# A selective scan between two routed layers: DMA transposes for the normalised rows, and one product in sixteen moved to VectorE

## The chip, the cores and the metric

One core of a Trainium2 chip runs the whole program. The metric is the device time in microseconds; lower is better. Engines are named as in the profile: PE (TensorE matmul), PEld (its weight loads), DVE (VectorE), ACT (ScalarE), POOL (GpSimd), SP (SyncE, which here only issues DMAs).

## The reference

The input x is 2 x 2048 tokens of 1024 channels. Three residual layers follow each other, each on a layer-normalised input:

```python
x = x + 0.5 * ffn(layernorm(x))
x = x + scan(layernorm(x))
x = x + 0.5 * ffn(layernorm(x))

def ffn(x):      # A 64 x 16 x 1024, B 64 x 1024 x 16, W 1024 x 1024
    vecs = einsum('arh,bsh->bsar', A, x)
    _, idx = top_k(norm(vecs, axis=-1), 4)
    routes = one_hot(idx, 64).sum(-2) / 4
    v = einsum('bsa,bsar->bsr', routes, vecs)
    return x @ W.T + bias + einsum('bsa,ajr,bsr->bsj', routes, B, v)

def scan(x):     # 16 states a channel
    delta_r, B_mat, C_mat = split(x @ W_xproj.T)             # 128, 16, 16
    delta = softplus(delta_r @ W_dt.T + b_dt)
    h[t] = exp(delta[t] * A) * h[t-1] + delta[t] * B_mat[t] * x[t]
    return sum over states (h * C_mat) + x * D_param
```

## The kernel before, in words

A unit is one of the two ffn layers on 128 tokens: 32 units of kind 1 (first ffn) and 32 of kind 2 (second), 64 in a row, numbered from 0. A planner (`plan`) sets their order once: kind 1 first, then a mix, as the scan's results come. The scan runs underneath, in units 3 to 59: its work is 1024 blocks, and `block_at` deals them out over twentieths of a unit, so each engine's `unit` function is a fixed list in which `scans(lo, hi)`, `decays(lo, hi)`, `loads(a, lo, hi)` and `states(a, third)` are set between the steps of the ffn. No engine reorders anything; each waits on semaphores in its list's order.

The ffn on PE. The rows are split into a high and a low f16 part (`xT[:, 0]`, `xT[:, 1]`), and so are the weights. Each of the three products (`experts` into pv, `base` and `routed` into po) is 2 halves of the columns x 24 matmuls of 128x512: the first two "thirds" are high rows by both weight parts, the last third is low rows by the high weights. In unit a, PE does base(a), routed(a), then experts(b) of the next unit b = a.after. ACT squares the experts' result, DVE sums, takes the top four and makes the routed rows (`gather`), SP turns them by a DMA transpose into uT (`turn`, L409).

The normalised rows of b before the change. DVE takes statistics (`unit_stats`), ACT finishes them (`prepare`) and writes xn in f32 (`normed`, L842). PE transposes xn in eight blocks into PSUM (`norm_blocks`, L552) after the second third of routed(a, 1). ACT copies each half of the result to f16 (`high`, L847), DVE subtracts it from the f32 one for the low part (`low_part`, L1094). The experts of b wait for both (L625, L626). The same transposes also serve the scan's input (`scan_blocks`) and, in kind 2, the scan's output (`y_blocks`).

The scan. A tile is 512 token-channel columns; a chunk is 2 or 4 token blocks (`SIZES`), with two or one part a tile. A block i is one of a tile's 16 states; a group G is four blocks, g = G % 4. For each block ACT computes exp(delta * A) into pA in PSUM, two buffers (`decay`, L942); for each group POOL multiplies delta*x by B into Hr (`times_b`, L512 and L518). DVE runs the scan in place (L1157), ACT keeps the last column (`keep_last`, L928), POOL multiplies the group's 2048 columns by C in place (`times_c`, L528), PE sums over states (`sum_states`, L727). Four Hr buffers go round. Delta and delta*x of the next tiles come over HBM by SP's spreads (L354, L361), which wait until decays or `times_b` have freed their buffers.

Of the kernel before, what the change touches and what calls it, by code (L numbers as in the profile page):

```python
# [12 lines left out]
AHEAD = 10  # L13
LEAD = 14
# [105 lines left out]
def build(nc, x, AT, BT, WT, bias, WxT, WdtT, b_dt, A_log, D_par, out):  # L120
# [41 lines left out]
    with ctx:  # L162
# [43 lines left out]
        pjs = xn[:, 0:NX]  # L206
        drs = auxs[:, 0:P]
# [55 lines left out]
        s_xT = sem("s_xT"); s_xhi = sem("s_xhi"); s_xlo = sem("s_xlo")  # L263
        s_vec = sem("s_vec"); s_sq = sem("s_sq"); s_n2 = sem("s_n2"); s_mk = sem("s_mk"); s_gm = sem("s_gm")
# [38 lines left out]
        def _(sp):  # L303
# [106 lines left out]

            def loads(a, lo, hi):
# [28 lines left out]
            def unit(l, a, b):  # L440
# [22 lines left out]
                loads(a, 9, 18)  # L463
# [20 lines left out]
        def _(pool):  # L484
# [36 lines left out]
            def times_c(G):  # L521
                g = G % 4
                c = chunk_of_tile[G // 4]
                pool.wait_ge(s_sv, G + 1)
                pool.wait_ge(s_ldc[g], 16 * (c.q + 1))
                h = split(Hr[:, G % NH, :, :].rearrange("p s t -> p (s t)"), c)
                by_c = Cr[:, g, 0:c.width].unsqueeze(1).broadcast_to([P, 4 * c.parts, c.width])
                pool.tensor_tensor(h, h, by_c, ALU.mult).then_inc(s_cm, 1)  # L528
# [18 lines left out]
        def _(pe):  # L547
# [20 lines left out]
            def norm_blocks(b, half):  # L568
                if half == 0:
                    pe.wait_ge(s_xn, b.u + 1)  # L570
                if half == 0:
                    pe.wait_ge(s_u, b.u * 2)
# [33 lines left out]
            def first_base(a):  # L606
# [10 lines left out]
                for k in range(KD):  # L617
                    pe.wait_ge(s_loW, k + 1)
                    for nb in range(2):
                        nc.tensor.matmul(po[:, nb, :], xT[:, 0, k, :], wW[:, 1, k, nb * HF:(nb + 1) * HF],  # L620
                                         start=False, stop=False)
# [9 lines left out]
            def base(a, nb, third):  # L631
# [7 lines left out]
                product(po[:, nb, :], xT, wW, nb, third, False, False)  # L639
# [92 lines left out]
            def unit(l, a, b):  # L732
# [61 lines left out]
            norm_blocks(US[0], 0)  # L794
            norm_blocks(US[0], 1)
# [5 lines left out]
        def _(act):  # L801
# [37 lines left out]
            def normed(b, nT):  # L839
                act.wait_ge(s_nT, nT)  # L840
                act.wait_ge(s_pq, nT // 2)
                nc.scalar.activation(xn[:, :], xin[:, b.p, :], ACT.Identity, scale=lnb["ln1"]["r"][:, :],  # L842
                                     bias=lnb["ln1"]["nm"][:, :]).then_inc(s_xn, 1)

            def high(b, half):
                act.wait_ge(s_xT, b.u * 2 + 1 + half)
                nc.scalar.activation(xT[:, 0, half * KB:(half + 1) * KB, :].rearrange("p k t -> p (k t)"), ptn[half],  # L847
                                     ACT.Copy).then_inc(s_xhi, 1)
# [16 lines left out]
            def normed2(a, xT_done):  # L865
                act.wait_ge(s_xT, xT_done)
# [55 lines left out]
            def keep_last(G):  # L922
# [3 lines left out]
                src = split(Hr[:, G % NH, :, :].rearrange("p s t -> p (s t)"), c)[:, :, c.width - 1]  # L926
                dst = hst[:, 16 * k:16 * (k + c.parts)].rearrange("p (k c) -> p k c", c=16)[:, :, 4 * g:4 * g + 4]
                nc.scalar.activation(dst, src.rearrange("p (s k) -> p k s", s=4), ACT.Copy).then_inc(s_sv, 1)  # L928
# [16 lines left out]
            def unit(l, a, b):  # L945
# [25 lines left out]
                decays(4, 7)  # L971
# [3 lines left out]
                delta_copy(a, 0)  # L975
                if late:
                    projection_copies(late)
                decays(8, 9)
                delta_out(a, 0)
                if b:  # L980
                    prepare(b)
                decays(9, 10)
                if b:
                    normed(b, 2 * (a.f1s - (a.kind == 1)))
                decays(10, 12)
                if b:
                    high(b, 0)
                if b:
# [321 lines left out]
```

## Time and profile before

| | |
|---|---|
| median of 3 runs | 2722.13 us (2721.1 to 2724.64) |
| the profiled execution, its own time | 2721.68 us |
| its span | 2719.8 us, granted clock 0.987 |
| DMA moved | 390.29 MB |

The page shows busy time, share of the span and instruction count of each engine; a group row shows the line, engine and tiles, the count, the busy time in all and the mean of one in ns, and then the idle time just before them and what ended it. A timeline row begins with start and length in us. Matmuls overlap: their length is longer than the distance at which they follow each other, so cost on PE is read from start to start. L numbers are lines of the kernel before.

### The profile page before, as it was taken

Reading aid. Unit: us, or ns where it says so; the run is one execution under the profiler, and the core shown is the slowest. Engines: PE = TensorE matmul, PEld = TensorE weight load, DVE = VectorE, ACT = ScalarE, POOL = GpSimd, SP = SyncE. Lnnn points to the kernel's source line nnn. Section 1 sums busy time; section 2 is a strip of 40 time slices with the busy share of each in tenths; the row PEclk is TensorE's granted clock in tenths of the full one; section 3 lists DMA queues with packets and bytes.
Section 4 is the critical chain, followed back from the end, with each engine's and each line's share of the span. In section 5 each row is a group of like instructions: output and inputs, shape, how many; then the busy total and the mean of one; then the engine's idle time right before and its main releaser. Section 6 shows DMA issues by size and latency. Waiting matters only on the chain.

```text
span 2719.8 us, 39965 instructions
## 1 busy us (share of the span) xinstructions
PE 2593.5 (95%) x13664; PEld 1178.2 (43%) x13664; DVE 2227.7 (82%) x2933; ACT 1505.0 (55%) x3363; POOL 2350.0 (86%) x703
## 2 busy tenths in 40 slices
PE   4989999999989999999999999999999999999999
PEld 1444444444434444444444444444444444444444
DVE  8448888888878898888888988888888889989943
ACT  5347666665545555555556555555555555656521
POOL 2138998899999999999998999999999999999910
PEclk8989999999999999999999999999999999999999
DMA  5145444644464454645454455544555455554321
GB/s 223 52 117 154 144 148 135 172 141 144 131 183 150 136 156 130 190 141 147 139 177 139 147 153 156 157 130 147 156 172 149 134 156 161 159 144 150 103 63 54
DMA packets 333217, 390.29 MB, mean 143 GB/s; under 512 B 149459, under 2 KB 249939, under 8 KB 333014
## 3 DMA queue, kind: packets, MB, share of 16 engines
q1 hardware_dynamic: 316118, 354.18, 43.8%
q10 hardware_dynamic: 16896, 33.56, 4.0%
q8 instruction: 108, 1.77, 0.3%
q14 instruction: 95, 0.78, 0.1%
HBM read 250.82 MB, written 103.29 MB: 130 GB/s over the span
## 4 chain that ended last, share of the span: by engine, by line
PE 57%; DVE 16%; POOL 6%; DMA 6%; issue 5%; ACT 4%; DVEq 4%; ACTq 1%; SPq 0%; POOLq 0%
PE po L560 20%; PE pv L560 9%; PE po L564 9%; DVE mreg L1157 7%; PE py L727 6%; PE pv L564 4%; POOL mreg L518 3%; PE pv L689 2%; POOL mreg L528 2%; DMA delta_scratch<-mreg 2%; DVE sel L1114 2%; PE pv L708 1%; PE pv L552 1%; DVEq L1116 1%; DMA uT<-sel 1%
## 5 line engine op out<-in xcount | busy, mean ns | idle before, releaser
L528 POOL TENSOR_TENSOR mreg<-mreg 128x2048 f32<-128x2048 f32 x256 | 1163.0, 4543 | 70.7 <-ACT hst L928 70.0
L1157 DVE TENSOR_TENSOR_SCAN mreg<-pA,hst,mreg 128x512 f32<-128x512 f32 (+1 forms) x1024 | 1048.9, 1065 | 50.2 <-ACT pA L942 43.8
L942 ACT ACTIVATE pA<-mreg,nA 128x512 f32<-128x512 f32 (+1 forms) x1280 | 744.4, 598 | 410.0 <-DVE mreg L1157 379.4
L518 POOL TENSOR_TENSOR mreg<-mreg 128x1024 f32<-128x1024 f32 x340 | 796.4, 2370 | 118.3 <-DMA mreg<-delta_scratch 103.8
L560 PE MATMUL po<-wB,uT 128*128 128x512 f16 x2016 | 471.0, 382 | 12.1 <-DVE xin L1080 7.5
L560 PE MATMUL po<-wW,xT 128*128 128x512 f16 x2016 | 474.5, 382 | 0.0
L560 PE MATMUL pv<-wA,xT 128*128 128x512 f16 x2016 | 461.1, 381 | 8.3 <-ACT mreg L911 7.2
L512 POOL TENSOR_TENSOR mreg<-mreg 128x2048 f32<-128x2048 f32 x86 | 390.2, 4537 | 4.0 <-issue 3.8
L560 PEld LDWEIGHTS pv<-wA,xT 128*128 128x128 f16 x2016 | 191.5, 98 | 284.5 <-issue 51.7
L560 PEld LDWEIGHTS po<-wB,uT 128*128 128x128 f16 x2016 | 193.4, 98 | 266.0 <-issue 48.3
L560 PEld LDWEIGHTS po<-wW,xT 128*128 128x128 f16 x2016 | 196.4, 99 | 250.2 <-issue 40.6
L727 PE MATMUL py<-mreg,Em 128*32 128x512 f32 (+1 forms) x2560 | 273.9, 518 | 6.3 <-DVE mreg L1168 6.1
L1157 DVE TENSOR_TENSOR_SCAN mreg<-pA,cst,mreg 128x256 f32<-128x256 f32 (+1 forms) x256 | 244.0, 997 | 15.7 <-ACT pA L942 14.1
L564 PE MATMUL po<-wB,uT 128*128 128x512 f16 x1008 | 238.4, 379 | 0.0
L564 PE MATMUL po<-wW,xT 128*128 128x512 f16 x1008 | 238.4, 379 | 0.0
L564 PE MATMUL pv<-wA,xT 128*128 128x512 f16 x1008 | 238.3, 379 | 0.0
L1098 DVE TENSOR_REDUCE n<-sel 128x32 f32<-128x512 f32 x128 | 87.5, 684 | 172.5 <-ACT sel L855 172.2
L1130 DVE SCALAR_TENSOR_TENSOR xin<-po,sc,xin 128x512 f32<-128x512 f32 x128 | 94.1, 735 | 85.6 <-PE po L564 82.0
L564 PEld LDWEIGHTS po<-wW,xT 128*128 128x128 f16 x1008 | 96.3, 98 | 132.8 <-issue 20.5
L564 PEld LDWEIGHTS pv<-wA,xT 128*128 128x128 f16 x1008 | 97.5, 98 | 125.7 <-issue 10.0
L564 PEld LDWEIGHTS po<-wB,uT 128*128 128x128 f16 x1008 | 96.2, 98 | 122.9 <-issue 21.3
L1071 DVE BATCH_NORM_STATS2 ln_st<-xin 128x6 f32<-128x512 f32 x192 | 122.7, 681 | 9.2 <-DMA xin<-x 3.0
(132 smaller groups left out, 2357.6 us busy)
## 6 DMA issues: line engine op xcount, KB each, us to landing
mreg<-delta_scratch SPq DMA_DIRECT2D x256, 512.0 KB, 5.1
mreg<-xnT_scratch SPq DMA_DIRECT2D x128, 256.0 KB, 5.2
delta_scratch<-mreg ACTq DMA_DIRECT2D x128, 256.0 KB
xin<-x SPq DMA_DIRECT2D x32, 512.0 KB, 4.7
x_scratch<-xin SPq DMA_DIRECT2D x32, 512.0 KB, 4.7
xnT_scratch<-auxs SPq DMA_DIRECT2D x32, 512.0 KB, 3.2
yT_scratch<-mreg SPq DMA_DIRECT2D x64, 256.0 KB, 4.9
uT<-yT_scratch SPq DMA_DIRECT2D x32, 512.0 KB, 6.1
```

Source lines behind the costliest of these rows:

```text
L512: pool.tensor_tensor(h, u, b.broadcast_to([P, 4 * c.parts, c.width]), ALU.mult).then_inc(s_bm, 2)
L518: pool.tensor_tensor(h[:, half * n:half * n + n, :], u, b.broadcast_to([P, n, c.width]), ALU.mult).then_inc(s_bm, 1)
L528: pool.tensor_tensor(h, h, by_c, ALU.mult).then_inc(s_cm, 1)
L560: last = nc.tensor.matmul(dst, lhs[:, 0, k, :], w[:, wb, k, nb * HF:(nb + 1) * HF], start=(first and k == 0 and wb == 0), stop=False)
L564: last = nc.tensor.matmul(dst, lhs[:, 1, k, :], w[:, 0, k, nb * HF:(nb + 1) * HF], start=False, stop=(stop and k == KD - 1))
L689: last = nc.tensor.matmul(pj[:, 0:NX], auxs3[:, k, :], wx[:, k, :], start=(k == 0), stop=(k == KD - 1))
L727: last = nc.tensor.matmul(split(py[32 * s:32 * s + 32, :], c)[:, n, :], Em[:, :], h[:, c.parts * s + n, :], start=(g == 0 and n == 0), sto ...
L942: last = nc.scalar.activation(dst[:, part, :], src[:, part, :], ACT.Exp, scale=nA[:, m:m + 1])
L1071: V.bn_stats(t["st"][:, 6 * n:6 * n + 6], src[:, n * HF:(n + 1) * HF])
L1098: V.tensor_reduce(n2[:, nb * NE // 2:(nb + 1) * NE // 2], sel3[:, nb * NE // 2:(nb + 1) * NE // 2, :], AX.X, ALU.add)
L1130: V.scalar_tensor_tensor(dst, po[:, nb, :], sc[:, 3:4], dst, ALU.mult, ALU.add).then_inc(s_res, 1)
L1157: last = V.tensor_tensor_scan(h, split(pA[:, i % 2, :], c)[:, part, :], h, before, ALU.mult, ALU.add)
```

## The change

1. The rows b are normalised by ACT twice: to f16 (`high_rows`, into xr, a view of xn in f16) and in f32 into PSUM (`full_rows`). DVE subtracts (`low_part`) into the second half of xr. SP turns both halves by DMA transposes into xT (`turn_rows`), between the loads of the scan; the high one after a new semaphore s_bs says that base(a) has read xT. PE's `norm_blocks` is left out, except for unit 0.
2. Of each tile's block 12 (first block of group g = GV = 3), DVE writes the scan into pA and multiplies it by C from there into Hr; POOL's `times_c` leaves this block out in that group; ACT keeps its last column by itself (`keep_first`).
3. ACT's and DVE's lists are reordered around this.

```diff
+GV = 3
+        xr = xn[:, :].bitcast(f16).rearrange("p (c n) -> p c n", c=2)
...
+            def turn_rows(b, part):
+                if part == 0:
+                    sp.wait_ge(s_bs, b.u)
+                    sp.wait_ge(s_xhi, b.u + 2)
+                else:
+                    sp.wait_ge(s_xlo, b.u * 2 + 2)
+                sp.dma_start_transpose(xT[:, part, :, :], xr[:, part, :]).then_inc(s_xc[part], 16)
...
-                loads(a, 9, 18)
+                if b:
+                    turn_rows(b, 0)
+                loads(a, 9, 11)
+                if b:
+                    turn_rows(b, 1)
+                loads(a, 11, 18)
...
+                first = c.parts if g == GV else 0
+                h = split(Hr[:, G % NH, :, :].rearrange("p s t -> p (s t)"), c)[:, first:, :]
+                by_c = Cr[:, g, 0:c.width].unsqueeze(1).broadcast_to([P, 4 * c.parts - first, c.width])
                 pool.tensor_tensor(h, h, by_c, ALU.mult).then_inc(s_cm, 1)
...
             def experts(b, nb, third):
                 if nb == 0 and third != 1:
-                    pe.wait_ge(s_xhi, b.u * 2 + 2)
-                    pe.wait_ge(s_xlo, b.u * 2 + (1 if third == 0 else 2))
+                    pe.wait_ge(s_xc[third // 2], 16 * b.u)
+                    pe.wait_ge(s_xlo, b.u * 2 + 1)
...
                 routed(a, 1, 1)
-                if b:
-                    norm_blocks(b, 0)
-                if b:
-                    norm_blocks(b, 1)
                 states(a, 10)
...
+            def high_rows(b, nT):
                 act.wait_ge(s_nT, nT)
                 act.wait_ge(s_pq, nT // 2)
+                act.wait_ge(s_xc[0], 16 * (b.u - 1))
+                act.wait_ge(s_xc[1], 16 * (b.u - 1))
+                nc.scalar.activation(xr[:, 0, :], xin[:, b.p, :], ACT.Identity, scale=lnb["ln1"]["r"][:, :],
+                                     bias=lnb["ln1"]["nm"][:, :]).then_inc(s_xhi, 1)
+
+            def full_rows(b, half):
+                act.wait_ge(s_u, b.u * 2)
+                nc.scalar.activation(ptn[half], xin[:, b.p, half * HF:(half + 1) * HF], ACT.Identity,
+                                     scale=lnb["ln1"]["r"][:, :], bias=lnb["ln1"]["nm"][:, :]).then_inc(s_xn, 1)
...
+            def keep_first(i):
+                act.wait_ge(s_sc, i + 1)
+                c, k = chunk_of_tile[i // 16], channels_at(i // 16)
+                src = split(pA[:, i % 2, :], c)[:, :, c.width - 1]
+                dst = hst[:, 16 * k:16 * (k + c.parts)].rearrange("p (k c) -> p k c", c=16)[:, :, i % 16]
+                nc.scalar.activation(dst, src, ACT.Copy)
+                act.drain()
+
             def decay(i):
                 if i % 4 == 1 and i > 4:
                     keep_last(i // 4 - 1)
+                if i % 16 == 4 * GV + 2 and i < 4 * NGRP:
+                    keep_first(i - 2)
...
-                decays(4, 7)
+                decays(4, 6)
+                delta_copy(a, 0)
+                delta_out(a, 0)
+                decays(6, 7)
                 if late:
                     projections(late)
                 decays(7, 8)
-                delta_copy(a, 0)
                 if late:
                     projection_copies(late)
-                decays(8, 9)
-                delta_out(a, 0)
                 if b:
                     prepare(b)
+                decays(8, 9)
+                if b:
+                    high_rows(b, 2 * (a.f1s - (a.kind == 1)))
                 decays(9, 10)
                 if b:
-                    normed(b, 2 * (a.f1s - (a.kind == 1)))
+                    full_rows(b, 0)
+                if b:
+                    full_rows(b, 1)
                 decays(10, 12)
-                if b:
-                    high(b, 0)
-                if b:
-                    high(b, 1)
...
+            def low_part(b, half):
+                dve.wait_ge(s_xn, b.u * 2 + 1 + half)
+                dve.wait_ge(s_xhi, b.u + 2)
+                dve.wait_ge(s_xc[1], 16 * (b.u - 1))
+                cols = slice(half * HF, (half + 1) * HF)
+                V.tensor_tensor(xr[:, 1, cols], ptn[half], xr[:, 0, cols], ALU.subtract).then_inc(s_xlo, 1)
...
+                    a = split(pA[:, i % 2, :], c)[:, part, :]
                     before = cst[:, 5:6] if c.fresh else hst[:, m:m + 1]
-                    last = V.tensor_tensor_scan(h, split(pA[:, i % 2, :], c)[:, part, :], h, before, ALU.mult, ALU.add)
+                    last = V.tensor_tensor_scan(a if i % 16 == 4 * GV else h, a, h, before, ALU.mult, ALU.add)
+                if i % 16 == 4 * GV:
+                    dve.drain()
+                    dve.wait_ge(s_ldc[GV], 16 * (c.q + 1))
+                    by_c = Cr[:, GV, 0:c.width].unsqueeze(1).broadcast_to([P, c.parts, c.width])
+                    last = V.tensor_tensor(split(Hr[:, G % NH, s, :], c), split(pA[:, i % 2, :], c), by_c, ALU.mult)
                 last.then_inc(s_sc, 1)
...
-                scans(4, 5)
                 delta(a, 0)
-                scans(5, 7)
+                scans(4, 6)
                 if b:
                     unit_stats(b)
-                scans(7, 9)
+                scans(6, 9)
                 result(a, 0)
-                scans(9, 11)
+                scans(9, 10)
                 if b:
                     low_part(b, 0)
-                scans(11, 12)
                 if b:
                     low_part(b, 1)
+                scans(10, 12)
                 delta(a, 1)
```

## Rows read from the trace of the kernel before

**Rows 1.** The page's busy table: busy us, share of the span, instructions.
```profile
PE 2593.5 (95%) x13664; PEld 1178.2 (43%) x13664; DVE 2227.7 (82%) x2933; ACT 1505.0 (55%) x3363; POOL 2350.0 (86%) x703
```
**Rows 2.** Windows view: stretch, its length, then each engine's busy time.
```profile
core 0: us, PE busy (x) PEld busy (x) DVE busy (x) ACT busy (x) POOL busy (x), PEclk, DMA share, GB/s
2257.70:2297.00 39.30, 38.97 (x200) 17.04 (x199) 35.71 (x44) 22.01 (x48) 39.30 (x13) 1.00 0.55 158
...
222.80:2590.50 2367.70, 2298.01 (x12256) 1037.67 (x12255) 2048.30 (x2659) 1382.77 (x3099) 2284.86 (x671) 0.99 0.50 149
2590.50:2719.80 129.30, 124.25 (x617) 58.31 (x615) 46.68 (x78) 18.37 (x48) 4.52 (x1) 1.00 0.19 51
```
**Rows 3.** Waits view of PE: total us, times, longest.
```profile
PE pv L708 <- DVE sel L1114: 26.3, 27, 2.7
PE pv L552 <- DVE sel L1125: 13.0, 20, 1.3
```
**Rows 4.** Timeline of PE, a unit without scans: start and length in us.
```profile
2647.69 0.60 PE L552 MATMUL pv<-idf,xn 128*128 128x128 f32 x4
...
2648.57 1.89 PE L564 MATMUL po<-wB,uT 128*128 128x512 f16 x8
```
**Rows 5.** Groups of the page, POOL: count, busy us, mean ns, idle before.
```profile
L528 POOL TENSOR_TENSOR mreg<-mreg 128x2048 f32<-128x2048 f32 x256 | 1163.0, 4543 | 70.7 <-ACT hst L928 70.0
...
L518 POOL TENSOR_TENSOR mreg<-mreg 128x1024 f32<-128x1024 f32 x340 | 796.4, 2370 | 118.3 <-DMA mreg<-delta_scratch 103.8
```
**Rows 6.** Groups view, all lines: operations like those added or removed.
```profile
L842 ACT ACTIVATE xn<-xin,ln_nm,ln_r 128x1024 f32<-128x1024 f32 x64 | 78.6, 1228 | 0.9
...
L928 ACT ACTIVATE hst<-mreg 128x4 f32<-128x4 f32 (+1 forms) x256 | 52.9, 206 | 105.7 <-DVE mreg L1157 103.7
...
L1143 DVE TENSOR_TENSOR mreg<-pv,mreg 128x512 f32<-128x512 f32 x64 | 44.3, 692 | 5.5 <-issue 0.9
L1094 DVE TENSOR_TENSOR xT<-pv,xT 128x512 f16<-128x512 f32 x64 | 44.1, 689 | 66.5 <-ACT xT L847 66.3
L1137 DVE TENSOR_TENSOR pv<-pv,mreg 128x512 f32<-128x512 f32 x64 | 43.4, 678 | 13.0 <-ACT pv L906 13.0
...
L906 ACT ACTIVATE pv<-mreg 128x512 f32<-128x512 f32 x64 | 38.5, 602 | 4.3
```
**Rows 7.** View of line 409, the DMA transposes of the routed rows.
```profile
DMA to landing us min/median/max: 3.0/3.2/8.1
```
**Rows 8.** DMA issues of the page: count, size, us to landing.
```profile
mreg<-delta_scratch SPq DMA_DIRECT2D x256, 512.0 KB, 5.1
```
**Rows 9.** Timelines of SP, ACT and PE in a unit with little slack.
```profile
2308.06 2.65 SPq L409 DMA_TRANSPOSE uT<-sel  x2
...
2319.12 0.87 ACT L942 ACTIVATE pA<-mreg,nA 128x256 f32<-128x256 f32 x2
2319.93 1.23 ACT L842 ACTIVATE xn<-xin,ln_nm,ln_r 128x1024 f32<-128x1024 f32 x1
...
2325.81 3.63 PE L560 MATMUL pv<-wA,xT 128*128 128x512 f16 x16
```
**Rows 10.** Timelines of SP and PE in the first unit with scans.
```profile
210.85 0.54 SPq L456 DMA_DIRECT2D bc_scratch<-auxs  x1
...
210.90 2.32 PE L560 MATMUL pv<-wA,xT 128*128 128x512 f16 x10
```
**Rows 11.** The chain that ended last, around 1722 us: start, length, what.
```profile
1722.08 8.14 DMA uT<-sel
...
1730.36 2.94 PE po L560 x8
```
**Rows 12.** Timelines of SP, ACT and POOL around 1520 us, a spread and its reader.
```profile
1522.32 16.57 SPq L361 DMA_DIRECT2D mreg<-delta_scratch  x2
...
1530.05 1.23 ACT L842 ACTIVATE xn<-xin,ln_nm,ln_r 128x1024 f32<-128x1024 f32 x1
...
1545.05 4.70 POOL L518 TENSOR_TENSOR mreg<-mreg 128x1024 f32<-128x1024 f32 x2
```

More of the change, by code:

```diff
@@ L263, in build @@
         s_xT = sem("s_xT"); s_xhi = sem("s_xhi"); s_xlo = sem("s_xlo")
+        s_xc = [sem(f"s_xc{n}") for n in range(2)]; s_bs = sem("s_bs")
         s_vec = sem("s_vec"); s_sq = sem("s_sq"); s_n2 = sem("s_n2"); s_mk = sem("s_mk"); s_gm = sem("s_gm")
@@ L619, in first_base @@
                     for nb in range(2):
[L620 to L621 removed]
+                        last = nc.tensor.matmul(po[:, nb, :], xT[:, 0, k, :], wW[:, 1, k, nb * HF:(nb + 1) * HF],
+                                                start=False, stop=False)
+                last.then_inc(s_bs, 1)
             def experts(b, nb, third):
                 if nb == 0 and third != 1:
[L625 to L626 removed]
+                    pe.wait_ge(s_xc[third // 2], 16 * b.u)
+                    pe.wait_ge(s_xlo, b.u * 2 + 1)
                 last = product(pv[:, nb, :], xT, wA, nb, third, True, True)
@@ L638, in base @@
                     nc.tensor.matmul(po[:, nb, :], onesb[:, :], brow[:, nb * HF:(nb + 1) * HF], start=True, stop=False)
-                product(po[:, nb, :], xT, wW, nb, third, False, False)
+                last = product(po[:, nb, :], xT, wW, nb, third, False, False)
+                if (nb, third) == (1, 2):
+                    last.then_inc(s_bs, 1)
             def first_routed(a):
@@ L837, in prepare, with first_normed, first_high @@
                 refine("ln1", 1)
-            def normed(b, nT):
+            def first_normed(b):
+                nc.scalar.activation(xn[:, :], xin[:, b.p, :], ACT.Identity, scale=lnb["ln1"]["r"][:, :],
+                                     bias=lnb["ln1"]["nm"][:, :]).then_inc(s_xn, 2)
+            def first_high(half):
+                act.wait_ge(s_xT, 1 + half)
+                nc.scalar.activation(xT[:, 0, half * KB:(half + 1) * KB, :].rearrange("p k t -> p (k t)"), ptn[half],
+                                     ACT.Copy).then_inc(s_xhi, 1)
+            def high_rows(b, nT):
                 act.wait_ge(s_nT, nT)
                 act.wait_ge(s_pq, nT // 2)
[L842 to L848, printed above, removed]
+                act.wait_ge(s_xc[0], 16 * (b.u - 1))
[6 more added lines that the diff above has]
+                                     scale=lnb["ln1"]["r"][:, :], bias=lnb["ln1"]["nm"][:, :]).then_inc(s_xn, 1)
             def squares(b, nb):
@@ L1010, in _ @@
             prepare(US[0])
-            normed(US[0], 0)
-            high(US[0], 0)
-            high(US[0], 1)
+            first_normed(US[0])
+            first_high(0)
+            first_high(1)
             act.wait_ge(s_scl, 1)
@@ L1086, in unit_stats, with first_low @@
                     dve.drain()
-                dve.wait_ge(s_xn, b.u)
+                dve.wait_ge(s_xn, b.u * 2)
                 stats("ln1", xin[:, b.p, :], s_mv)
-            def low_part(b, half):
-                dve.wait_ge(s_xhi, b.u * 2 + 1 + half)
+            def first_low(half):
+                dve.wait_ge(s_xhi, 1 + half)
                 hi = xT[:, 0, half * KB:(half + 1) * KB, :].rearrange("p k t -> p (k t)")
```

30 lines of the change are left out of this document (14 added, 16 removed).

## The prediction

> **What bounds the kernel now.** I read the page's busy table first: TensorE (PE) is busy 95% of the span [rows 1]. That alone could still be waits, so I cut the span with the windows view. Before 222.8 us the kernel loads, splits weights and fills the scan pipeline; after 2590.5 us no scans are left. In the 2367.7 us between, PE is busy 2298.0 and GpSimd (POOL) 2284.9: 97.1% and 96.5%. VectorE (DVE) has 2048.3 (86.5%), ScalarE 1382.8 (58%); in single units POOL is busy without a gap, 39.30 of 39.30 us [rows 2]. Two engines are full and a third is near. Which of the two sets the end is told by their waits. PE's largest steady waits are for DVE's routed rows, 26.3 and 13.0 us in all, and no row of the view has PE waiting for POOL [rows 3]; POOL's L528 waited 70.0 us for the saved ends of the scans [rows 5]. So PE walks nearly through its own list, with POOL beside it. A change that relieves only one of them would be stopped by the other; this one relieves both.
>
> **PE: the turned rows.** Per unit, eight 128x128 transposes of the normalised rows go. In a unit without scans they start at 2647.69 and the next product at 2648.57: 0.88 us for eight [rows 4]. The first unit keeps them, so 63 x 0.88 = 55 us leave PE's list. Nothing is added to it.
>
> **POOL: three blocks in place of four in every fourth group.** A multiply of 2048 elements takes 4543 ns, one of 1024 takes 2370 [rows 5]; the slope is 2.12 ns an element, so 1536 elements cost about 3.46 us, 1.09 less. 64 of the 256 groups have g = 3: 64 x 1.09 = 70 us leave POOL, more than PE's 55, so POOL doesn't become the bound by this.
>
> **DVE: the product it takes over.** It multiplies a 512-wide block in PSUM by C into SBUF. L1143 is the same form: 692 ns [rows 6]. 64 x 0.69 = 44 us more busy time. The scan's end is signalled only after it, so the decay two blocks on comes later: behind the product ScalarE copies the last column (0.21, L928) and computes the decay (0.87 for two halves [rows 6, 9]), while DVE has one scan of about 1.3 to run. With drains and two hand-overs that is a stall of 0 to 0.5 us. I take 1.0 us a tile in all, 64 us; the ends are 44 and 76. That the scan writes PSUM instead of SBUF is shown by no row; the nearest pair is L1137 into PSUM (678) and L1143 into SBUF (692) [rows 6], so I price it at nothing.
> What pays for it: DVE now waits 66.3 us for the high half before L1094 (the chain PE transpose, ScalarE copy, DVE) [rows 6]. In the new order ScalarE writes the high and the full rows itself and DVE reads them a scan or two later, so I let that wait go whole. Net about zero for DVE, which has 2367.7 - 2048.3 = 320 us idle in the middle.
>
> **ScalarE.** Out: one pass of 1.23 (L842) and two copies of about 0.6. In: one 1024-wide pass into f16 (1.23 by L842) and two 512-wide ones into PSUM (0.60 by L906) [rows 6]. The same. The single-column copies add 64 x 0.21 and their drains, some 25 us on an engine that is 42% idle: nothing.
>
> **The DMA transposes: 126 more, two a unit.** The kernel already turns the routed rows so, same size and type. The data land 3.2 us after issue in the median, 3.0 at best, 8.1 at worst [rows 7], and SP is held 2.65 us by a pair [rows 9]. Do they arrive in time? Take a tight unit. ScalarE ended the normalised rows at 2321.16 (2319.93 + 1.23) and the experts' products began at 2325.81 [rows 9]. In the new order the high rows come one decay earlier, in the place of the decay at 2319.12, so they end about 2320.4; issued 2320.5, landed 2323.7. The products, 0.88 earlier, want to start at 2324.9. Margin 1.2 us; where ScalarE isn't pushed so late it is 2 to 3. The low rows: the full rows end 1.2 to 2 us behind the high ones, two subtractions of 0.69 follow, then SP: issued near 2324, landed near 2327.5. They are needed only by the last third, after 16 products (3.63 us [rows 9]): about 2328.4. Margin about 1. So I expect no steady wait, and short ones in two kinds of place:
> (1) Where SP itself is late. In the first scanning unit SP reached the new transpose's place only at 211.39 (end of L456), when PE began the experts at 210.90 [rows 10]. With 3.2 us of landing and products that want to start at 210.0, PE waits 4.6 us. Two more units of the filling are half as bad: together 8.
> (2) Where a new chunk's loads stand ahead. The routed rows have such a landing: 8.14 us on the chain, and PE then ran eight products in 2.94 us [rows 11], where sixteen take 3.63 elsewhere, so it came out of the wait at the lower clock level. Some six borders; I take 1 us each, 6.
>
> **SP's queue.** turn_rows stands ahead of the loads of the unit's second half and waits for ScalarE. Behind it lie the spreads. Around 1520 SP issued the first of two from 1522.32 on, while the high rows would be there only at about 1530; it moves 9 us, to 1531.6, and to 1534.6 if the second transpose stands ahead of it too. Its reader on POOL starts at 1545.05 [rows 12], and a spread lands in 5.1 us [rows 8]: 1539.7, 5 us early. Its twin wasn't issued before 1538, when POOL released the buffer, and doesn't move. I followed the other units' spreads in the same way; none runs out of slack, so this costs nothing; if the transposes came more than 5 us later, each us over would be a us of POOL's.
>
> Here a rule speaks against the edit. The trace shows 3.2 us for a whole 128x1024 set, eight blocks, by DMA, and 0.88 by PE [rows 4, 7]. The Trainium skill, "VectorE: DVE Perf Modes", section "The three transpose paths", gives 390 ns a 128x128 block on TensorE and 1309 ns on the DMA crossbar, and its rules prefer TensorE where PSUM will do as the destination. By that price eight blocks in a row would be an estimated 10.5 us, and in the tight unit the experts would wait some 6 us. The landings in the trace disagree with it, and the sum goes by the trace.
>
> **The sum.** The profiled execution is 2721.7 us (the span of 2719.8 and 1.9 around it), 0.4 under the median of 2722.1. 2721.7 - 55 + 8 + 6 = 2681; POOL (-70) is no bar to it and DVE none. PE's own 39 us of waits for DVE [rows 3] should move little: POOL's lead helps, DVE's longer list hurts; I take 2 off for them: **2679**.
>
> **Rivals.**
> *A, the forecast*: 2660 to 2700.
> *B, a deeper gain.* POOL was in truth the pacer, and PE's 39 us of waits come from scans that POOL held up. Then half of those go as well, and landings cost nothing: 2679 - 20 - 14 = 2645. For it: POOL without a gap in [rows 2]; against: DVE's list grows.
> *C, DVE becomes the bound.* The 66 us wait only moves (DVE waits for the full rows as it did for the high ones), and most of the products' 64 us stand unhidden, say 45: 2681 + 45 = 2726, about no change. For it: DVE is 87% full and works in order, and the loop of scan and decay has little slack; against: its 320 us idle.
> *D, slower: the experts wait for the turned rows in every unit.* The place is PE at the first or the last third of the experts. It decides once landing and SP's lateness together exceed the margin of 1 to 2.5 us steadily, for instance if a transpose beside a spread lands in 5.5 rather than 3.2. At 2 us a unit, 63 x 2 - 55 = +71: 2793; at 1.2 us some 2742. Against: today's transposes have the same spreads beside them and a median of 3.2. The page's price is the hard form of it.
> *E, the spreads come late and POOL starves*: every second tile 2.5 us, 32 x 2.5 = 80: 2759.
>
> **Chances.** A 0.60, B 0.13, C 0.11, D 0.12 (0.02 of it by the page's price), E 0.04. A measurement tells 0.2% (5.4 us) from nothing. Faster: A, B and a third of C, 0.77; within 0.2%: the middle of C and the mild edge of D, 0.06; slower 0.17. The predicted time is 2679. The range takes in most of B and of C: 2648 to 2732; the likeliest case alone is 2660 to 2700.
>
> **What would show it.** PE: no L552 from xn but for the scan inputs and the first unit, busy about 55 us less. POOL: 64 instructions of 128x1536 at 3.4 to 3.5 us, busy 2280. DVE: 64 products of 0.69, busy about 2275, the wait before the low part under 15 us. The new transposes land in 3.2 in the median, and PE waits for DMA into xT under 20 us, most of it before 360 us and at chunk borders. Wrong, if the waits view has PE waiting for xT in most units (D), ScalarE's decays and PE both waiting more for a DVE above 93% (C), or POOL waiting for DMA from the delta scratch (E).

## The result: 0.2% slower

| | before | after |
|---|---|---|
| median, 20 runs each | 2721.68 us | 2726.41 us |
| ratio after/before, 95% interval | | 1.002, 1.0012 to 1.0029 |
| span of the profiled execution | 2719.8 us | 2721.0 us |

The change takes 4.7 us more, where 43 less were forecast. In the experiments below one execution of kernel 7 took 8630 us at a granted clock of 0.34 and is left out: the median is 2692.9 by the other three, 2694.7 with it. First the page's busy table, and the row of the DMA queue of SP (packets, MB, share of 16 engines), of the kernel after:

```profile
PE 2548.2 (94%) x13160; PEld 1119.4 (41%) x13160; DVE 2259.2 (83%) x2997; ACT 1539.3 (57%) x3427; POOL 2279.8 (84%) x703
...
q1 hardware_dynamic: 449174, 387.23, 52.7%
```

Against [rows 1] PE lost 45 us and POOL 70, as the change meant, and DVE gained 31. The queue had 316118 packets and a share of 43.8% before: 126 transposes brought 133056 packets, 1056 each, and 8.9% of 2721 us, some 1.9 us of all 16 engines for each 256 KB.

The middle stretch (columns as in [rows 2]):

```profile
222.80:2590.50 2367.70, 2257.44 (x11805) 985.59 (x11802) 2079.27 (x2724) 1417.16 (x3172) 2216.75 (x671) 0.99 0.60 162
```

PE, 97.1% busy there before, is 95.3% busy, POOL falls from 96.5% to 93.6%. No engine is full any more, and the kernel isn't faster. The waits views of PE, POOL and DVE say what they wait for instead:

```profile
PE pv L726 <- DVE sel L1160: 38.1, 31, 3.1
PE pv L577 <- DMA xT<-xn: 37.3, 20, 8.2
PE pv L569 <- DVE sel L1171: 12.6, 19, 2.3
...
PE pv L581 <- DMA xT<-xn: 9.8, 9, 2.7
```
```profile
POOL mreg L545 <- ACT hst L955: 136.0, 66, 4.6
```
```profile
DVE mreg L1204 <- ACT pA L980: 83.7, 53, 5.0
...
DVE pA L1204 <- ACT pA L980: 10.7, 4, 3.5
```

PE waits 47.1 us for turned rows, which is new, and 50.7 for the gather (39.3 in [rows 3]). Two steps of PE's list wait for it: `z`, the small product that a tile's delta is made from (L726), and `y_blocks` (L569). POOL's wait for the scans' last columns has doubled from 70.0 [rows 5], and DVE's for decays grew from 57.9 (95 times) to 94.4 (57 times). Put start to start over all of PE's instructions, the time beyond the usual distance in pauses above 0.75 us went from 83.0 to 125.9 us, the extra length of products at the lower clock from 11.9 to 15.8, the time before the products of unit 1 from 95.9 to 101.4, and the rest of PE's list from 2524.9 to 2473.6. That is +42.9 + 3.9 + 5.5 - 51.3 = +1.0, the difference of the two spans but for 0.2. The 5.5 are the change's too: PE waits 3.68 us for the first turned rows of all, where it waited 1.07 for the low part before, and then runs sixteen products in 6.27 us in place of 3.61:

```profile
88.54 6.27 PE L577 MATMUL pv<-wA,xT 128*128 128x512 f16 x16 [3.68 <-DMA xT<-xn]
```

The groups of the new and changed operations, forms kept apart:

```profile
L545 POOL TENSOR_TENSOR mreg<-mreg 128x1536 f32<-128x1536 f32 x64 | 220.8, 3450 | 48.3 <-ACT hst L955 48.3
...
L1209 DVE TENSOR_TENSOR mreg<-pA,mreg 128x512 f32<-128x512 f32 x64 | 44.3, 692 | 4.8
L1204 DVE TENSOR_TENSOR_SCAN mreg<-pA,hst,mreg 128x512 f32<-128x512 f32 x600 | 738.1, 1265 | 50.7 <-ACT pA L980 50.6
L1204 DVE TENSOR_TENSOR_SCAN pA<-pA,hst,mreg 128x512 f32<-128x512 f32 x40 | 51.1, 1277 | 8.5 <-ACT pA L980 8.5
L1140 DVE TENSOR_TENSOR xn<-pv,xn 128x512 f16<-128x512 f32 x63 | 42.1, 669 | 2.2 <-ACT pv L872 2.2
L872 ACT ACTIVATE pt<-xin,ln_nm,ln_r 128x512 f32<-128x512 f32 x63 | 48.1, 763 | 0.0
```

On the engines every duration came out as priced but one (the writes into PSUM from `xin` take 763 ns, not 600: 20 us more on ScalarE). The durations of the engines' instructions are not where the forecast failed.

DVE no longer waits for the high half (66.3 us in [rows 6], 2.2 now), but its waits for decays grew. Most of them have one place. ScalarE's `prepare` (L832 to L846, some 2.3 us) now stands one decay earlier in its list, and in the trace 39 of the 57 waits, 66.6 of the 94.4 us, are for one of the decays right behind it; before, 23 waits and 10.4 us were. One of them:

```profile
2364.59 0.28 ACT L846 ACTIVATE ln_nm<-ln_nm,ln_t 128x1 f32<-128x1 f32 x1
2364.99 0.87 ACT L980 ACTIVATE pA<-mreg,nA 128x256 f32<-128x256 f32 x2
2365.90 1.39 DVE L1204 TENSOR_TENSOR_SCAN mreg<-pA,hst,mreg 128x256 f32<-128x256 f32 x2 [0.83 <-ACT pA L980]
```

Kernels 1, 6 and 7 below have the new order without a product on DVE, and there these waits come to 101 to 108 us; kernels 2, 11 and 14 have the old order, and there it is 40 to 51. So they come with parts 1 and 3 of the change, the rows' new way and the new order, and not with the product. What they cost in time no run shows: none has the new order alone.

Now the view of the new transposes' line:

```profile
L420 SPq DMA_TRANSPOSE xT<-xn x126: 1232/1250/5437, 85.5 to 2682.4; - x126
...
DMA to landing us min/median/max: 3.0/3.8/9.4
```

Median 3.8 where 3.2 was taken [rows 7]. A tenth of the first transposes of a unit needs 6.6 us or more. One late unit, in the timeline:

```profile
2360.06 0.68 SPq L357 DMA_DIRECT2D mreg<-delta_scratch  x1
2365.80 1.23 ACT L867 ACTIVATE xn<-xin,ln_nm,ln_r 128x1024 f16<-128x1024 f32 x1
2367.10 1.32 SPq L420 DMA_TRANSPOSE xT<-xn  x1
2368.75 1.90 PE L581 MATMUL po<-wB,uT 128*128 128x512 f16 x8
2374.22 5.20 PE L577 MATMUL pv<-wA,xT 128*128 128x512 f16 x16 [3.57 <-DMA xT<-xn]
```

ScalarE's rows are ready at 2367.0 and SP issues at 2367.1; PE stands from about 2370.6 and waits 3.57 us. Then sixteen products take 5.20 where they take 3.63 in [rows 9], 1.6 us more: the granted clock of their first 3.4 us is 0.52, the lower level (1.2 GHz). The windows view compares this landing with one in a unit without scans:

```profile
2367.10:2374.10 7.00, 3.55 (x28) 1.23 (x26) 6.92 (x12) 5.06 (x13) 4.99 (x3) 1.00 1.03 123
2644.60:2647.66 3.06, 3.06 (x16) 1.38 (x15) 0.35 (x1) 1.46 (x3) 0.00 (x0) 1.00 0.45 86
```

The last two columns are the DMA share and GB/s. All 16 DMA engines are full for 7 us and move only 123 GB/s; alone the same transpose lands in 3.06 at a share of 0.45.

### The profile page after: what moved, and what is told of

It reads as the page before. It is cut to its first block, busy times and chain, and to the rows that moved or that the text cites. A ratio compares the mean times of both kernels' runs of the same rounds, so it can differ in the third digit from the quotient of the medians.

```text
span 2721.0 us, 39559 instructions
## 1 busy us (share of the span) xinstructions
PE 2548.2 (94%) x13160; PEld 1119.4 (41%) x13160; DVE 2259.2 (83%) x2997; ACT 1539.3 (57%) x3427; POOL 2279.8 (84%) x703
## 3 DMA queue, kind: packets, MB, share of 16 engines
q10 hardware_dynamic: 16896, 33.56, 3.9%
## 4 chain that ended last, share of the span: by engine, by line
PE 34%; DVE 26%; DMA 8%; issue 8%; DVEq 8%; ACT 7%; POOL 5%; ACTq 2%; SPq 1%; POOLq 0%
DVE mreg L1204 11%; PE po L577 10%; PE pv L577 8%; PE po L581 5%; PE pv L581 4%; DMA xT<-xn 4%; PE py L745 3%; POOL mreg L534 2%; DVE sel L1160 2%; DMA delta_scratch<-mreg 2%; PE pv L707 2%; DVEq L1162 2%; DVE pv L1163 2%; POOL mreg L545 2%; ACT pA L980 2%
## 5 line engine op out<-in xcount | busy, mean ns | idle before, releaser
L545 POOL TENSOR_TENSOR mreg<-mreg 128x2048 f32<-128x2048 f32 (+1 forms) x256 | 1091.4, 4264 | 136.1 <-ACT hst L955 136.0
L1204 DVE TENSOR_TENSOR_SCAN mreg<-pA,hst,mreg 128x512 f32<-128x512 f32 (+1 forms) x960 | 978.9, 1064 | 64.7 <-ACT pA L980 64.5
L534 POOL TENSOR_TENSOR mreg<-mreg 128x1024 f32<-128x1024 f32 x340 | 794.3, 2359 | 124.1 <-DMA mreg<-delta_scratch 105.7
L577 PE MATMUL pv<-wA,xT 128*128 128x512 f16 x2016 | 468.8, 386 | 40.1 <-DMA xT<-xn 37.3
L528 POOL TENSOR_TENSOR mreg<-mreg 128x2048 f32<-128x2048 f32 x86 | 389.7, 4532 | 4.4 <-issue 4.3
L581 PE MATMUL pv<-wA,xT 128*128 128x512 f16 x1008 | 238.8, 380 | 9.9 <-DMA xT<-xn 9.8
L1144 DVE TENSOR_REDUCE n<-sel 128x32 f32<-128x512 f32 x128 | 87.5, 684 | 191.5 <-ACT sel L880 191.2
L1204 DVE TENSOR_TENSOR_SCAN mreg<-pA,cst,mreg 128x256 f32<-128x256 f32 (+1 forms) x240 | 228.1, 997 | 19.9 <-ACT pA L980 19.2
L880 ACT ACTIVATE sel<-pv 128x512 f32<-128x512 f32 x128 | 75.5, 590 | 138.6 <-PE pv L581 134.4
```

The lines of the kernel that those rows point to most:

```text
L528: pool.tensor_tensor(h, u, b.broadcast_to([P, 4 * c.parts, c.width]), ALU.mult).then_inc(s_bm, 2)
L534: pool.tensor_tensor(h[:, half * n:half * n + n, :], u, b.broadcast_to([P, n, c.width]), ALU.mult).then_inc(s_bm, 1)
L577: last = nc.tensor.matmul(dst, lhs[:, 0, k, :], w[:, wb, k, nb * HF:(nb + 1) * HF], start=(first and k == 0 and wb == 0), stop=False)
L581: last = nc.tensor.matmul(dst, lhs[:, 1, k, :], w[:, 0, k, nb * HF:(nb + 1) * HF], start=False, stop=(stop and k == KD - 1))
L880: nc.scalar.activation(sel[:, nb * HF:(nb + 1) * HF], pv[:, nb, :], ACT.Square).then_inc(s_sq, 1)
L1144: V.tensor_reduce(n2[:, nb * NE // 2:(nb + 1) * NE // 2], sel3[:, nb * NE // 2:(nb + 1) * NE // 2, :], AX.X, ALU.add)
```

## The experiments

Each ran beside the kernel before on the same chip (before: 2720.7 to 2722.7 us in all); times are medians, and the ratio and its 95% interval are against the kernel before. Waits are those of one profiled execution. It can lie some us off the median: it took 2718.0 us in kernel 8 (median 2713.3), 2752.8 in kernel 10 (2741.1) and 2705.1 in kernel 13 (2712.6). First the two parts one by one.

**1. Transposes alone.** The changed kernel, all products by C on POOL.

> The DMA transposes of the rows alone, all products by C on POOL again. Theory L (the turned rows land late): PE's list is 55 us shorter, PE waits for DMA into xT some 45 us as in the changed kernel, POOL's list is 70 us longer again and 96% full: 2720 to 2740. Theory V (VectorE's product and its drain give back what PE gained): without them the gain shows, 2675 to 2700, and PE's waits for the routed rows fall from 38 to about 26 us.

2728.3 us, 1.0018 (1.0006 to 1.003). **2. Product alone**, in the kernel before.

> The kernel before with only the product moved: PE transposes stay. Theory L: PE's list is unchanged and sets the end, 2712 to 2724, POOL's busy time falls by 70 us for nothing. Theory V: DVE's longer loop holds PE up, its waits for the routed rows grow by 12 us or more and POOL's for the scan ends double: 2730 to 2750.

2726.0 us, 1.0012 (1.0003 to 1.0021). Each part alone makes it slower by as much as both together. In kernel 1 PE's waits for the gather are 32.5 us and those for turned rows 56.2; in kernel 2 the gather is waited for as long as in the changed kernel, 50.5 us (39.3 before), so that growth comes with the product:

```profile
PE pv L710 <- DVE sel L1128: 36.5, 35, 2.6
PE pv L554 <- DVE sel L1139: 14.0, 20, 2.1
```

POOL's waits for the last columns are 83.2 us in kernel 1 and 116.4 in kernel 2: much of their doubling is only the time that POOL no longer works. Kernel 2's time fits neither theory's range.

**3. Transposes issued by ScalarE's queue**, so that SP's list can't delay them.

```diff
-                if b:
-                    turn_rows(b, 0)
...
                 if b:
+                    turn_rows(b, 0)
                     full_rows(b, 0)
...
+                if b:
+                    turn_rows(b, 1)
```

> The changed kernel with the two transposes a unit issued from ScalarE's queue in place of SP's. If they land late because they stand behind the spreads in SP's list and queue (L, order), landings go to about 3.2 us at all percentiles, PE's waits for xT fall from 47 to under 10 us, ScalarE's list is held 2.5 us a unit: 2680 to 2700. If it is the 16 DMA engines that are shared (L, bandwidth), landings stay at 3 to 7.7 us and the time within 5 us of 2725. Theory V: 2720 either way.

2765.4 us, 1.016 (1.0137 to 1.0182). Landing, from the view of that tile, and waits of PE:

```profile
DMA to landing us min/median/max: 3.0/4.2/12.3
```
```profile
PE pv L564 <- DMA xT<-xn: 47.8, 24, 4.5
```

Another queue lands no sooner (median 4.2 against 3.8), and PE's waits for turned rows grow to 64.6 us, so SP's own delay alone isn't the cause. That the rest is the sharing of the 16 DMA engines is argued from their share of 1.03 above. ScalarE is held 1.27 us by each issue; neither theory had the 39 us that this kernel takes more than the changed one.

**4. No transposes**: PE reads a slice of wB in place of xT in `experts` and `base` (same shapes, other data; the products with the rows are left out). **5.** The same, transposes issued but unread.

```diff
-                sp.dma_start_transpose(xT[:, part, :, :], xr[:, part, :]).then_inc(s_xc[part], 16)
...
-                last = product(pv[:, nb, :], xT, wA, nb, third, True, True)
+                last = product(pv[:, nb, :], still, wA, nb, third, True, True)   # still = wB[:, :, :, 0:P]
```

> The changed kernel without the two DMA transposes; PE's products with the normalised rows read a fixed slice of wB in place of xT, so their result is left out of the computation, the instruction counts stay. No wait for xT, no transfer, SP free. Theory L: nearly all of the 55 us shows, 2662 to 2680. Theory V: VectorE's list is the same as in the changed kernel, so 2700 to 2725.

> As e4 (PE reads a fixed slice of wB in place of xT), but the two DMA transposes are issued at their places from SP and land in xT, and PE doesn't wait for them. Only their traffic and SP's holding remain. Theory W (what the transposes cost is PE's wait for them): as e4, 2698 to 2706. Theory T (traffic: spreads land later, SP is blocked and POOL and VectorE wait for their inputs): 2712 to 2726.

2701.9 us, 0.992 (0.9904 to 0.9936), and 2704.0, 0.9931 (0.9916 to 0.9945). The traffic and SP's part cost 2.2 us, which four executions each don't tell from nothing; PE's waiting for the rows costs 22.4.

**6. As 4, block 12's product left out on both engines. 7. The changed kernel, that product left out on both.**

> As e4, and the product by C of block 12 is left out altogether, on VectorE and on POOL. If VectorE's product took the 35 us that e4 was short of the forecast, 2662 to 2680, with PE's wait for the routed rows at L721 of e4 back from 47 to about 25 us. If something else in the new order of the lists took them, 2690 to 2705.

> The changed kernel with the product by C of block 12 left out on both engines; the DMA transposes stay. Against e4 and e6 it tells whether the two costs add. If they add: 2720 to 2727 less what e6 gains over e4 (20 to 35), 2690 to 2705. If the waits for xT hide what the product costs: 2715 to 2727.

2672.8 us, 0.9812 (0.9796 to 0.9828), and 2692.9, 0.989 (0.987 to 0.991). PE's wait for the gather in kernel 4, then in 6:

```profile
PE pv L721 <- DVE sel L1152: 46.8, 37, 3.0
```
```profile
PE pv L721 <- DVE sel L1150: 30.4, 33, 2.7
```

The product on DVE costs 29.1 us without transposes and 33.5 with them, with all that comes with it: the scan into pA, the drain and ScalarE's own copy. Kernel 1 has the product on POOL and takes 35.4 more than kernel 7: what POOL was relieved of, DVE's load takes back. So the product costs 29 to 35 us on either engine, and moving it brings nothing.

**8. z of position 0 behind base(a,1,0)** in the changed kernel.

```diff
-                z(a, 0)
                 states(a, 2)
                 base(a, 1, 0)
+                z(a, 0)
```

> The changed kernel with PE's z product of position 0 moved behind the first third of base(a, 1). PE waits 38 us for the routed rows ahead of it (31 times): the place has 1.9 us more cover. If the in-order wait of PE for VectorE's gather is where the product's cost enters, that wait falls under 15 us and the time to 2700 to 2712; if the delay only moves to the next wait of PE (y_blocks, or the delta chain), no change, 2720 to 2727.

2713.3 us, 0.997 (0.9958 to 0.9982), a little above the range. `z` waits for the gather (semaphore s_gm) and PE works in its list's order; 1.9 us of base(a,1,0), and about 1 of states where there are any, now stand ahead of it. PE's waits for the gather fall from 50.7 to 30.8 us, and nearly all of them have moved to `y_blocks`:

```profile
PE pv L569 <- DVE sel L1171: 29.5, 31, 2.6
```

**9. Statistics, rows and transposes a twentieth earlier. 10. The same with z moved.**

> The changed kernel with statistics, high, full and low rows and both transposes one twentieth of a unit (about one scan block, 1.9 us) earlier on all engines' lists. If the 22 us that PE's waiting for xT costs are a matter of lateness, PE's wait for xT falls from 47 to about 20 us and the time to 2708 to 2716. If ScalarE's chain (it waits for the scan's projections in units with a late input) or SP's own lateness holds the rows where they are: 2720 to 2727.

> e9 and the z product of position 0 behind base(a, 1)'s first third (as in e8) together. If both are waits of their own that add: 2713 less 12 to 18, so 2695 to 2702. If one takes the other's slack: 2706 to 2714.

2750.3 us, 1.0106 (1.0092 to 1.012), and 2741.1, 1.0069 (1.0055 to 1.0083). Waits of PE, then of DVE, in kernel 9:

```profile
PE pv L726 <- DVE sel L1159: 45.8, 35, 3.1
PE pv L577 <- DMA xT<-xn: 27.9, 10, 8.8
```
```profile
DVE mreg L1203 <- ACT pA L980: 121.0, 55, 4.1
DVE xn L1139 <- ACT pv L872: 37.1, 6, 9.6
```

Both forecasts missed. The rows did come sooner (PE waits 29.1 us for them in place of 47.1), but ScalarE made them ahead of decays, and DVE paid with the scan: its waits for decays are 132 us in place of 94, and 89 of them are for the decay right behind the high rows. Earlier isn't free in this loop.

**11. z moved in the kernel before.**

> The kernel before with only the z product moved as in e8. PE waited 26 us there before. If PE is the bound of the kernel before, those 26 us go and it gets 8 to 15 us faster: 2707 to 2715. If POOL, full in most units, is as much a bound, nothing: 2719 to 2724. If it is as fast as e8, the move of z is worth the same in both and the change itself still brings nothing.

2700.6 us, 0.992 (0.9906 to 0.9933): faster than both, and than each range. PE's waits for the gather shrink from 39.3 to 27.0 us, POOL's for scan ends from 70.0 to 54.3. The span falls by 19.4 us, more than these 12.3; PE's busy time falls too, from 2593.5 to 2585.1, with the same 13664 instructions, and why it does no run shows.

**12. The product deferred**: kernel 8, block 12 scanned into Hr, its product made there after scan 13.

```diff
-                    last = V.tensor_tensor(split(Hr[:, G % NH, s, :], c), split(pA[:, i % 2, :], c), by_c, ALU.mult)
-                last.then_inc(s_sc, 1)
...
+                last.then_inc(s_sc, 1)
+                if i % 16 == 4 * GV + 1:
...
+                    h12 = split(Hr[:, G % NH, s - 1, :], c)
+                    V.tensor_tensor(h12, h12, by_c, ALU.mult)
```

> e8 with VectorE's product taken out of the loop of scan and decay: block 12 is scanned into Hr as the others, its end is signalled at once, ScalarE saves its last column, and VectorE multiplies it in Hr (both inputs in SBUF) only after scan 13. The same 44 us of work. If the product's cost is the drain and the hand-over (the decay of block 14 coming late), 10 to 20 us under e8: 2693 to 2703. If it is VectorE's time as such: 2710 to 2716. If two SBUF inputs on VectorE slow POOL down, POOL's multiplies grow beyond 4.54 us and the time is over 2716.

2810.9 us, 1.0321 (1.0306 to 1.0335). Its group row:

```profile
L1211 DVE TENSOR_TENSOR mreg<-mreg 128x512 f32<-128x512 f32 x64 | 171.4, 2678 | 5.3 <-ACT hst L963 5.1
```

It tested something else than meant: the same product takes 692 ns with one input in PSUM and 2678 with both in SBUF beside a busy POOL. The Trainium skill, "GPSIMD Engine Reference", section "Specifications", says that GpSimd's SBUF interfaces are shared with VectorE, with contention for instructions of VectorE that have two SBUF inputs. This trace agrees by these two durations; no run has such a product beside an idle POOL. The third branch of the forecast had the place right and the engine wrong: VectorE's product grew, POOL's multiplies of 2048 elements hardly did (4584 ns, 4535 in the changed kernel).

**13. The same DVE time outside the hand-over**: kernel 7 with an unread reduction of 512 elements (660 ns in its trace, 42.2 us in all) right after scan 12 has been signalled.

```diff
                 last.then_inc(s_sc, 1)
+                if i % 16 == 4 * GV:
+                    V.tensor_reduce(amx[:, 0:4], idf[:, :].unsqueeze(1).broadcast_to([P, 4, P]), AX.X, ALU.max)
```

> Turned rows as in the changed kernel, the product by C of block 12 left out on both engines, and in its place a VectorE reduction of 128x512 elements that nobody reads, issued right after scan 12 has been signalled: so much VectorE time as the product took, but outside the hand-over from scan to decay. The kernel without the product took 2694.7, the changed kernel 2726.4. If the product costs because the next decay and scan wait for it (the hand-over), 2695 to 2703. If it costs because VectorE has 44 us more to do and every gather and scan behind it is that much later, 2715 to 2726.

2712.6 us, 0.9968 (0.9957 to 0.9979): neither. Over kernel 7's 2692.9 DVE's time costs 19.7; the product inside the hand-over, with its own copy on ScalarE, costs 13.8 more. This kernel's executions spread from 2705 to 2724 us, so the split is good to a few us.

**14. The product on DVE in kernel 11** (before, z moved).

> The kernel before with z of position 0 moved behind base(a,1,0) (2700.6) and the product of block 12 on VectorE; rows still turned by TensorE. Before, the product alone cost 4.3 us; with the rows turned by DMA and z moved the kernel took 2713.3. If the cost of the whole change that is left with z moved (12.6 us) is TensorE's waits for the turned rows, this one takes 2699 to 2705. If it is the product, 2709 to 2714 (above it, if TensorE's eight transposes each unit had given the gather time).

2699.7 us, 0.9917 (0.9904 to 0.993): with z out of its way, too, moving the product from POOL to DVE changes nothing (-0.9). It doesn't say what the product costs here, as no kernel with z moved leaves it out on both engines. In the kernel before the move cost 4.3 us; that these came through PE's wait for the gather fits, but the difference is hardly larger than the intervals. Kernel 8 takes 13.6 us more than this one: that belongs to turning the rows by DMA and the new order of the lists together.

**15. Half of y_blocks behind base(a,1,1) too**, in kernel 11. What the expectation calls the attention output is the scan's output.

> The kernel before with z of position 0 moved, as in the run of 2700.6, and the second half of the transposes of the attention output moved behind base(a,1,1), so that TensorE has 7 us more work ahead of its last wait for the gather (26.3 us in 32 places). If TensorE's in-order wait is still the bound: 2675 to 2690. If the scan loop and VectorE's rows behind them are the bound by now: 2697 to 2703; above 2703 if add_y behind the later transposes holds VectorE's scans.

2713.0 us, 0.996 (0.9948 to 0.9972), above both ranges. Of the waits for the gather 1.8 us are left, but the wait only moved; the view of PE's waits has now

```profile
PE po L560 <- DMA uT<-sel: 47.8, 29, 3.5
```

PE gets to `routed` before the routed rows have landed. After z's move the next thing late is the chain behind the gather, and this much work moved in front of it doesn't help.

**16. SP's turn_rows ahead of two blocks of spreads**, in the changed kernel.

```diff
-                loads(a, 2, 9)
+                loads(a, 2, 7)
...
-                loads(a, 9, 11)
+                loads(a, 7, 10)
```

> The changed kernel with SP's two transposes of the rows two and one blocks of spreads earlier in its queue (behind the spreads of stretch 6 in place of 8), nothing else moved. If the late landings come from spreads issued just ahead of them, TensorE's 47 us of waits for turned rows fall to some 25 and the time to 2705 to 2715. If instead SP now waits for ScalarE's rows with spreads behind it, the decays and scans wait for their data: 2726 to 2760.

2713.1 us, 0.9966 (0.9956 to 0.9976). The transposes land in 3.3 us in the median in place of 3.8, and PE's waits for them fall from 47.1 to 36.0 us, not to 25.

**17. The same with z moved. 18. As 17, all products on POOL.**

> The changed kernel with both mends: SP's transposes of the rows ahead of two blocks of spreads (alone 2713.1 where the changed kernel takes 2726.4) and z of position 0 behind base(a,1,0) (alone 2713.3). If they mend two different waits of TensorE (landings, gather), they add up: 2697 to 2703. If TensorE, freed of the one, only meets the scan loop a little later, 2708 to 2714.

> As the run with both mends, but all products by C on POOL as before: the DMA transposes alone, mended. In the changed kernel moving the product or not made no difference (2728.3 against 2726.4), in the kernel before with z moved none either (2699.7 against 2700.6). If POOL and VectorE still trade one for one: within 4 us of the run with both mends. If the mends take TensorE's waits away and POOL's blocks (4.5 us each) become the bound: 6 to 20 us longer than it.

2698.4 us, 0.9921 (0.9905 to 0.9937), and 2703.7, 0.9934 (0.9917 to 0.995). PE's waits for turned rows in kernel 16, then the waits of PE in 17:

```profile
PE pv L577 <- DMA xT<-xn: 24.7, 7, 8.3
...
PE pv L581 <- DMA xT<-xn: 11.3, 15, 3.2
```
```profile
PE pv L569 <- DVE sel L1171: 30.1, 31, 2.8
PE pv L713 <- ACT xn L904: 21.0, 19, 2.0
PE pv L577 <- DMA xT<-xn: 20.9, 8, 8.1
```

Of the first transposes' waits 13 of 20 are gone; those of the second rose from 9 to 15. The two mends add up: 13.3 for the queue, 13.1 for z (kernel 8), 28.0 together. Kernel 18 takes 5.3 us more than 17, between its two ranges and within the intervals of both: again moving the product tells little. 17 beats before and after, but not 11 and 14, which need no DMA transposes for the rows: 2698.4, 2700.6 and 2699.7 are one time within their intervals.

## Why the prediction was wrong

It named 2679, faster; the time is 2726, where its rival C stood, but by C and a part of D together. Two steps of it failed: DVE's product was taken as paid by the 66 us wait, and the landings as giving no steady wait. The runs make this ledger, each step one difference of medians (-57 is the 55 of PE's list and the 2 of its waits):

| step | us | forecast |
|---|---|---|
| before | 2721.7 | 2721.7 |
| eight PE transposes gone, POOL without block 12 (6) | -48.9 | -57 |
| the product on DVE (4 less 6) | +29.1 | 0 |
| transposes issued (5 less 4) | +2.2 | 0 |
| PE waits for them (after less 5) | +22.4 | +14 |
| after | 2726.4 | 2679 |

The ledger depends on the order of its steps. Its first step takes block 12's product away from both engines, which the change doesn't do. Taken the other way, kernel 1 first, the transposes alone come to +6.6 us, where -41 was forecast, and moving the product then to -1.9. What holds either way: the product costs 29 to 35 us wherever it stands, and issuing the transposes and waiting for them 20.1 us without the product (7 less 6) and 24.6 with it.

- *PE: 63 x 0.88 = 55 leave the list.* Right: the rest of PE's list fell by 51.3, the unit without scans from 33.9 to 33.0.
- *POOL: 70 us.* Right (2350.0 to 2279.8; 3450 ns against 3.46). "No bar" was too little said: kernels 1 and 7 differ by 35 us for it. POOL's relief would have been worth half its size, had DVE not taken the work.
- *DVE: product +64, paid by the 66 us wait, net about zero.* **This step failed, and is the largest: 29.1 us (33.5 with the transposes) in place of 0.** The product's 692 ns and the 44 us were right, and the wait did go (66.3 to 2.2). But the payment didn't come: DVE's waits for decays rose from 57.9 to 94.4 us, most of it behind `prepare`, and in kernel 1, without the product, to 108.1. That is rival C's "only moves", to another place than it named. And the product makes PE wait longer for the gather in every pair of kernels that differ by it: 39.3 to 50.5 us before (kernel 2), 42.4 to 61.0 (6 to 4), 33.9 to 50.7 (7 to after). The 320 us of idle time didn't help: 191.2 us of DVE's waits in the changed kernel are for the squares of the experts' result, in a place of their own. Kernel 13 says by which way the product costs: about 20 us by DVE's plain length and 14 by the hand-over.
- *PE's waits for DVE: 2 off.* Wrong in sign: 39.3 to 50.7. I had read [rows 3] as a small remainder. Kernel 11 shows what it hid: 2 to 3 us of other work ahead of the 27 waits of `z` gave back 21.1 us, though the waits for the gather shrank by 12.3 only.
- *Landings: no steady wait, 8 + 6.* **Mis-sized.** PE's waits for turned rows cost 22.4 us against 14 (24.6 with the issuing), and stand at 47.1 in the view. The filling has 15.9 of them against 8, and elsewhere: 3.7 at the first turned rows of all, where nothing was priced, 0.6 in the unit priced at 4.6, 3.4 in a later one, and 8.2 in the unit ahead, whose transpose was issued 4.3 us late, behind eight spreads of the first chunk's B and C, and landed 9.1 after that. The rest isn't at borders alone. I took the median of today's transposes, which stand where the queue is calm; the new ones stand right behind `spread_inputs` and `spread_delta`. There the landing was off: PE waits for the first transpose in 20 of 63 units. Kernel 16, which moves only the place in the queue, gives back 13.3. How much of the rest is other traffic, how much the transposes' own load on the 16 engines, wasn't separated.
- *The SP queue costs nothing.* Right as far as spreads go: POOL's wait for the delta scratch is 105.7 against 103.8, and all but 1.4 and 4.3 us of it is one wait at the start (104.3 and 99.5).
- *The price weighed, 1309 ns a block* (the Trainium skill, "VectorE: DVE Perf Modes", section "The three transpose paths"): by it an estimated 10.5 us for eight. In the last five units, without scans, the first transpose lands in 3.0 to 3.1; the slowest of all takes 9.4. Multiplied by eight the price is wrong as a latency, but the preference for TensorE held here: turned by DMA the rows never beat the eight transposes of 0.88 us (14 against 8; 17 is level with 14).

What stays open: what the new order of ScalarE's and DVE's lists costs by itself, as no kernel has it alone; why kernel 6 is still 8 us short of its forecast; and why 11, 14 and 17 meet at 2700 though PE's list is 50 us shorter in 17 and POOL's 70 us in 14 and 17. That the loop of gather, routed rows, experts and top four sets the unit there is argued from kernel 15 and from 17's waits, not shown by a run.

## What to carry over

Here two engines were 97% busy and a third stood at 87%. The short waits of the fullest one, multiplied by how often they come, pointed at what was worth mending (21 us by moving `z`), while in the changed kernel 51 us cut from its list only let it reach the next wait sooner. Take a landing time from transfers at the same place of the queue, not from the median of all, and look at what is issued in the 10 us before. And a wait that goes from one engine's row counts as gain only after you have looked where else in the new order that engine will wait: a step moved one decay earlier on ScalarE gave DVE a new wait in 39 places. Work that two nearly full engines trade costs about the same on either.

## What the hardware showed that I had not expected

- A DMA transpose of 128x1024 f16 takes 1056 packets and about 1.9 us of all 16 engines, where ScalarE's queue (33.56 MB at 3.9% of 2721 us) takes 0.83 for as many bytes; it lands in 3.0 us alone and in up to 9.4 (12.3 from ScalarE's queue) beside other traffic, and holds its issuer 1.25 us (SP; 1.27 on ScalarE).
- A VectorE product with both inputs in SBUF took 2678 ns beside POOL, 692 with one in PSUM.
- PE is granted the lower clock level after a wait of 3.57 us: sixteen products in 5.20 us for 3.63, granted clock 0.52 in the first 3.4 us.
